# The down projection of each expert step is made between its two up projections instead of behind both

## The chip, the core and the metric

The kernel runs on one core of a Trainium2 chip. The metric is the device time of one execution in microseconds (us); the times given are medians of several executions of the same program. TensorE (PE in the profile) multiplies matrices, VectorE (DVE) and ScalarE (ACT) work element by element and copy results out of the accumulator banks (PSUM), GpSimd (POOL) issues the indirect transfers, SyncE (SP) the others.

## The reference

A block of three layers on x (8 sequences, 512 tokens, width 128): half an expert layer, a recurrent mixing layer, half an expert layer again.

```python
def _L0_ffn_ref(x, gate_w, w1, w3, w2):
    logits = jnp.einsum('btd,de->bte', x, gate_w)
    probs = jax.nn.softmax(logits, axis=-1)
    expert_weights, expert_indices = jax.lax.top_k(probs, TOP_K)          # TOP_K = 2 of E = 8
    expert_weights = expert_weights / expert_weights.sum(-1, keepdims=True)
    for i in range(E):
        wi = jnp.where(expert_indices == i, expert_weights, 0.0).sum(-1)
        h = silu(jnp.einsum('btd,df->btf', x, w1[i])) * jnp.einsum('btd,df->btf', x, w3[i])   # F = 512
        out = out + jnp.einsum('btf,fd->btd', h, w2[i]) * wi[..., None]
    return out

def _L0_attn_ref(x, ...):
    # x mixed with the token before it, three projections k, v, r, a scan over the tokens
    # with running maximum, numerator and denominator (_wkv), then
    return jnp.einsum('bsd,ed->bse', r * wkv, Wo)

x = x + 0.5 * _L0_ffn_ref(_layernorm(x), ...)
x = x + _L0_attn_ref(_layernorm(x), ...)
x = x + 0.5 * _L0_ffn_ref(_layernorm(x), ...)
```

## The kernel before

Each token goes to 2 of 8 experts. The kernel sorts the tokens by expert: GpSimd scatters their rows to `rows_in` in device memory, in tiles of 128 rows that belong to one expert each, and later gathers the results from `rows_out`. There are 177 such tiles, in nine runs (a run is a group of sequences, first for the first expert layer, then for the second). Each tile is one **step** t of the program, and all engines walk through the steps in the same order (`in_order`, L423): `tile(t)`, and behind it the extra steps that a planner (`make_plan`, L217) put behind tile t: norms, gating, counting and the whole mixing layer, cut in pieces.

What each engine does in step t, in the order of its queue:

- **TensorE** (`tile`, L1274): waits for `h` of step t-2; up projection with w1 into bank `pa` (`up`, L1236); turns the rows of the next load into `pT`, if the next step begins one (`turn_tile`, L1227); up projection with w3 into bank `pb`; down projection of step t-3 (SKEW is 3) into bank `py` (`down`, L1250), which first waits for s_yrow, that is for ScalarE's copy of the previous down projection. Then its extra steps: the k, v, r products (`project`, L1292), turns, gate logits, counts.
- **ScalarE** (`tile`, L792): copies `py` of step t-4 to `yrow` (`copy_y`, L780); copies `pT` to `rT` (L773); makes `sil` of `pa` (L798); issues the store of `yrow` to `rows_out` (L785). Then its extra steps: norms (`xn`), their high halves (`parts`), copies of the products (`kk`, `vv`, `tr`), `xT`, `xnT`, `logit`, and two exponentials (L862, L863).
- **VectorE** (`tile`, L1108): `h` = `sil` times `pb`, once both are there and the down projection of six steps ago has read its slot. Then its extra steps, up to several us of them.

`pa` and `pb` have two banks each, `py` has one. In the weights, an up projection is three float16 products for each piece (high and low parts), 12 matmuls of 128 columns, or 6 of 256 where two tiles share an expert (a paired step); a down projection is 4 float32 matmuls, each of which runs as two in the trace (8). At the start of a run TensorE loads the experts' offsets into registers (`load_experts`, L1264). After the last step TensorE waits for the last `h` and makes the last three down projections.

Of the kernel before, what the change touches and what calls it, by code (L numbers as in the profile page):

```python
# [152 lines left out]
def expert_of(t):  # L153

    run = max(r for r in range(RUNS) if START[r] <= t)
    return ESTART[run] + (TILE_OF[t][0] - QSTART[run] if PAIRS[run] else t - START[run])


def paired(t):

    return TILE_OF[t][2] == 2 and PAIRS[max(r for r in range(RUNS) if START[r] <= t)] > 0
# [250 lines left out]
def run_of(t):  # L412

    return max(r for r in range(RUNS) if START[r] <= t)


def wait(eng, sem, value):

    if not isinstance(value, int) or value > 0:
        eng.wait_ge(sem, value)  # L420
# [19 lines left out]
def macaron_kernel(nc, x, channel_vecs, att_w, gate, w1, w3, w2, out):  # L440
    with ExitStack() as ctx:
# [3 lines left out]
        def ps(name, shape, dt=F32):  # L445
            return ctx.enter_context(nc.psum_tensor(name, shape, dt))

        def sem(name):
            return ctx.enter_context(nc.semaphore(name))
# [85 lines left out]
        pb = [ps(f"pb{q}", [P, FC * T]) for q in range(2)]  # L535
# [41 lines left out]
        s_up3 = sem("w3_up_done")  # L577
# [44 lines left out]
        def _(sp):  # L622
# [64 lines left out]
            for t in range(TILES + SKEW + 1):  # L687
                if t < TILES and TILE_OF[t][1] == 0 and TILE_OF[t][0] + SLOTS < QSTART[RUNS]:
                    load(TILE_OF[t][0] + SLOTS)
                if t > SKEW:  # L690
                    sp.wait_ge(s_yrow, t - SKEW)
                if t < len(later):
                    fill(*later[t])
                for _, name, run, b in (p for p in PLAN if p[0] == t < TILES):
                    step(name, run, b)
# [187 lines left out]
        def _(dve):  # L883
# [119 lines left out]
            def place_on(run):  # L1003

                new, _, low, base, more = (ne[:, i, :] for i in range(5))
                at = count(B_STEPS, ("count", run, 0))
                dve.wait_ge(s_bfull, at)
                dve.tensor_tensor(new, bkB[:, 0:E], left[:, 1, :], ALU.subtract).then_inc(s_bread, 1)
                dve.wait_ge(s_bread, at)
                link(dve.tensor_scalar(nei[:, 0, :], new, 0.0, float(T - 1), ALU.max, ALU.add))  # L1010
                link(dve.tensor_scalar(neh[:, 0, :], nei[:, 0, :], T.bit_length() - 1, None, ALU.logical_shift_right))
                dve.tensor_copy(ends[:, 2, 0:1], ends[:, 1, E:])
                link(dve.tensor_copy(kp[:, 0, :], neh[:, 0, :]))
                link(dve.tensor_tensor_scan(ends[:, 2, 1:], one_s[:], kp[:, 0, :], 0.0, ALU.mult, ALU.add))
                link(dve.tensor_scalar(ends[:, 2, 1:], ends[:, 2, 1:], ends[:, 1, E:], None, ALU.add))
                link(dve.tensor_scalar(low, ends[:, 2, 0:E], float(T), None, ALU.mult))
                link(dve.tensor_tensor(base, low, left[:, 1, :], ALU.subtract))
                link(dve.tensor_tensor(more, left[:, 0, :], base, ALU.subtract))
# [204 lines left out]
        def _(pe):  # L1223
# [3 lines left out]
            def turn_tile(q):  # L1227
                pe.wait_ge(s_rin[q % SLOTS], 16 * (q // SLOTS + 1))
                wait(pe, s_rT, q)
                for n in range(TILE_OF[FIRST_STEP[q]][2]):  # L1230
                    for part in range(2):
                        mm = pe.transpose(pT[:, part, n * T:(n + 1) * T],  # L1232
                                          rin[:, q % SLOTS, n, part * D:(part + 1) * D], ident16[:])
                mm.then_inc(s_turn, 1)

            def up(t, bank, w):  # L1236

                q, half, _ = TILE_OF[t]
                per, own = (FC // 2, slice(0, 2 * T)) if paired(t) else (FC, slice(half * T, (half + 1) * T))
                cols = own.stop - own.start  # L1240
                for i in range(per):
                    c = half * per % FC + i
                    for k, (wp, xp) in enumerate(((0, 0), (0, 1), (1, 0))):
                        at = 2 * ((w + wp) * F + c * P)
                        mm = pe.matmul(bank[:, i * cols:(i + 1) * cols],  # L1245
                                       weight_bytes[:, bass.ds(experts[expert_of(t)] * 4 + at, 2 * P)].bitcast(F16),
                                       rT[:, q % 2, xp, own], start=(k == 0), stop=(k == 2))
                return mm

            def down(t):  # L1250

                q, block, _ = TILE_OF[t]
                cols, per = (2 * T, FC // 2) if paired(t) else (T, FC)
                wait(pe, s_yrow, t)
                for c in range(FC):
                    w = weight_bytes[:, bass.ds(experts[expert_of(t)] * 4 + 4 * (UPW + c * D), 4 * D)].bitcast(F32)
                    at = c % per * cols + (block * T if paired(t) else 0)
                    step = FIRST_STEP[q] + c // per if paired(t) else t
                    mm = pe.matmul(py[:], h[:, step % RING, at:at + T], w, start=(c == 0), stop=(c == FC - 1))  # L1259
                mm.then_inc(s_y, 1)  # L1260
# [3 lines left out]
            def load_experts(run):  # L1264

                pe.wait_ge(s_eid, run + 1)
                _, found = nc.values_load_multi_w_load_instructions(
                    eid[0:1, ESTART[run]:ESTART[run + 1]], engines=(mybir.EngineType.PE,), min_val=0,
                    max_val=(E - 1) * WORDS,
                    skip_runtime_bounds_check_because="tiles() writes a count of experts, at most E - 1, times WORDS")  # L1270
                for k in range(NE[run]):
                    experts[ESTART[run] + k] = found[k]

            def tile(t):  # L1274
                q, half, _ = TILE_OF[t]
                if t in START:
                    load_experts(run_of(t))
                if half == 0:
                    pe.wait_ge(s_rT, q + 1)
                wait(pe, s_h, t - 1)  # L1280
                up(t, pa[t % 2], 0).then_inc(s_up1, 1)
                if t + 1 < TILES and TILE_OF[t + 1][1] == 0:
                    turn_tile(TILE_OF[t + 1][0])
                up(t, pb[t % 2], 2).then_inc(s_up3, 1)
                if t >= SKEW:
                    down(t - SKEW)

            def bank_free(s_read, uses):

                wait(pe, s_read, uses - 1)  # L1290
# [68 lines left out]
            def weights_in():  # L1359
                turn_tile(0)  # L1360
                pe.wait_ge(s_uplo, E)
                pe.wait_ge(s_w2, 16 * E)

            in_order(tile, step, before_tiles=weights_in)
            pe.wait_ge(s_h, TILES)
            for t in range(TILES - SKEW, TILES):
# [28 lines left out]
```

## Time and profile before

| | |
|---|---|
| median of 3 runs | 621.75 us (621.48 to 623.04) |
| the profiled execution | 623.24 us, of which the span of its instructions is 621.4 us |
| TensorE busy | 521.1 us (84%) |
| VectorE, ScalarE, GpSimd busy | 423.8 us (68%), 318.9 us (51%), 389.3 us (63%) |
| mean granted TensorE clock | 0.97 of full speed |

How to read it: the steps begin at about 55 us, after the first routing and the loading of weights, and TensorE's last down projection starts at 596.7 us. The rest is the last gathers, their addition and the writing out. A busy share is a mean over stretches with different limits, so what a new order does is read from single steps and from the waits. In the profile, a time in brackets behind an instruction is the time for which its engine was idle before it, and what ended that. Starts are counted from the beginning of the span. The engine named PEld is TensorE's loading of weights, which overlaps its matmuls.

### The profile page before, as it was taken

Reading aid. Unit: us, or ns where it says so; the run is one execution under the profiler, and the core shown is the slowest. Engines: PE = TensorE matmul, PEld = TensorE weight load, DVE = VectorE, ACT = ScalarE, POOL = GpSimd, SP = SyncE. Lnnn points to the kernel's source line nnn. Section 1 sums busy time; section 2 is a strip of 40 time slices with the busy share of each in tenths; the row PEclk is TensorE's granted clock in tenths of the full one; section 3 lists DMA queues with packets and bytes.
Section 4 is the critical chain, followed back from the end, with each engine's and each line's share of the span. In section 5 each row is a group of like instructions: output and inputs, shape, how many; then the busy total and the mean of one; then the engine's idle time right before and its main releaser. Section 6 shows DMA issues by size and latency. Waiting matters only on the chain.

```text
span 621.4 us, 18551 instructions
## 1 busy us (share of the span) xinstructions
PE 521.1 (84%) x5866; PEld 477.7 (77%) x5866; DVE 423.8 (68%) x1218; ACT 318.9 (51%) x703; POOL 389.3 (63%) x490
## 2 busy tenths in 40 slices
PE   1235899999999899998999959998989999989930
PEld 1233789898978789877898849887879899978930
DVE  4862863556878988799998955887788765215431
ACT  5433674444585565756676534776473444434410
POOL 1171058489999970599808996003949887835973
PEclk9999899999999999999999979999998999989985
DMA  8963233544232221212221133111121442313332
GB/s 284 329 192 113 61 92 114 156 137 124 79 116 65 78 74 53 74 60 73 78 66 53 59 101 87 49 37 36 54 81 57 121 112 83 103 45 99 91 89 59
DMA packets 89062, 59.55 MB, mean 96 GB/s; under 512 B 10256, under 2 KB 82704, under 8 KB 88976
## 3 DMA queue, kind: packets, MB, share of 16 engines
q1 hardware_dynamic: 55296, 29.97, 16.5%
q0 software_dynamic: 8192, 16.79, 8.9%
q10 hardware_dynamic: 25488, 11.61, 6.5%
q8 instruction: 58, 0.95, 0.6%
q14 instruction: 28, 0.23, 0.1%
HBM read 28.65 MB, written 29.69 MB: 94 GB/s over the span
## 4 chain that ended last, share of the span: by engine, by line
PE 56%; DVE 13%; ACT 11%; issue 8%; POOL 8%; DMA 3%; POOLq 0%; ACTq 0%; DVEq 0%; SPq 0%
PE py L1259 18%; PE pa L1245 14%; PE pb L1245 12%; POOL rows_in L725 3%; ACT xn L817 3%; POOL yg L737 3%; DVE h L1114 3%; PE pT L1232 2%; PE bkB L1318 2%; PE bkB L1297 2%; ACT sil L798 2%; POOL pace L754 2%; PE bkA L1312 2%; ACT rT L778 1%; PE bkA L1297 1%
## 5 line engine op out<-in xcount | busy, mean ns | idle before, releaser
L725 POOL DMA_INDIRECT rows_in<-parts,slot x128 | 135.0, 1054 | 183.1 <-DVE slot L1039 161.2
L1114 DVE TENSOR_TENSOR h<-sil,pb 128x512 f32<-128x512 f32 x177 | 120.7, 686 | 127.3 <-ACT sil L798 79.6
L1259 PE MATMUL py<-ffn_w,h 128*128 x1416 | 198.6, 284 | 9.4 <-ACT yrow L783 9.0
L1259 PEld LDWEIGHTS py<-ffn_w,h 128*128 128x128 f32 x1416 | 175.2, 195 | 15.2 <-issue 12.3
L1245 PE MATMUL pa<-rT,ffn_w 128*128 128x128 f16 (+1 forms) x1752 | 151.7, 233 | 22.8 <-issue 12.5
L1245 PE MATMUL pb<-rT,ffn_w 128*128 128x128 f16 (+1 forms) x1752 | 154.5, 232 | 0.0
L1245 PEld LDWEIGHTS pa<-rT,ffn_w 128*128 x1752 | 124.2, 99 | 37.6 <-issue 26.4
L737 POOL DMA_INDIRECT yg<-rows_out,slot x128 | 125.4, 980 | 38.6 <-issue 22.8
L754 POOL MEMSET pace<- 128x544 uint8 x223 | 127.7, 573 | 0.1
L1245 PEld LDWEIGHTS pb<-rT,ffn_w 128*128 x1752 | 122.2, 98 | 6.8
L798 ACT ACTIVATE sil<-pa 128x512 f32<-128x512 f32 x177 | 105.3, 595 | 40.4 <-PE pa L1245 39.9
L783 ACT ACTIVATE yrow<-py 128x128 f32<-128x128 f32 x177 | 48.5, 274 | 87.2 <-PE py L1259 84.7
L778 ACT ACTIVATE rT<-pT 128x512 f16<-128x512 f16 (+1 forms) x112 | 56.8, 507 | 68.0 <-PE pT L1232 62.8
L1232 PE MATMUL pT<-ident,rin 128*128 128x128 f16 x354 | 38.6, 221 | 9.7 <-DMA rin<-rows_in 9.7
L817 ACT ACTIVATE xn<-xres,shift,rstd 128x128 f32<-128x128 f32 x96 | 39.3, 486 | 9.5 <-DVE shift L926 8.3
L1124 DVE SCALAR_TENSOR_TENSOR xres<-yg,wts,xres 128x128 f32<-128x128 f32 x120 | 34.1, 346 | 9.2 <-DMA yg<-rows_out,slot 8.6
L1312 PE MATMUL bkA<-ident,xn 128*128 128x128 f32 x64 | 11.8, 315 | 28.3 <-ACT xn L817 27.5
L1232 PEld LDWEIGHTS pT<-ident,rin 128*128 128x128 f16 x354 | 25.9, 99 | 11.0 <-DMA rin<-rows_in 10.0
L1312 PEld LDWEIGHTS bkA<-ident,xn 128*128 128x128 f32 x64 | 8.5, 165 | 29.6 <-issue 28.4
L904 DVE BATCH_NORM_STATS2 stats<-xres 128x6 f32<-128x128 f32 x96 | 20.9, 280 | 4.3 <-DMA xres<-in_x 3.9
L1297 PE MATMUL bkB<-xT,qkv_w 128*128 128x512 f16 x96 | 23.4, 379 | 0.3 <-ACT xT L847 0.3
L934 DVE TENSOR_TENSOR parts<-xn,parts 128x512 f16<-128x512 f32 x24 | 16.4, 689 | 10.6 <-ACT parts L831 10.5
(156 smaller groups left out, 459.2 us busy)
## 6 DMA issues: line engine op xcount, KB each, us to landing
rows_out<-yrow ACTq DMA_DIRECT2D x177, 64.0 KB, 1.9
rin<-rows_in SPq DMA_DIRECT2D x65, 128.0 KB
rows_in<-zrow SPq DMA_DIRECT2D x34, 128.0 KB, 2.0
shared<-in_w SPq DMA_DIRECT2D x16, 256.0 KB, 6.7
rin<-rows_in SPq DMA_DIRECT2D x47, 64.0 KB
rows_in<-zrow SPq DMA_DIRECT2D x2, 1472.0 KB, 11.0
xres<-in_x SPq DMA_DIRECT2D x4, 512.0 KB, 6.3
ffn_w<-in_w SPq DMA_DIRECT2D x8, 256.0 KB, 5.2
```

Source lines behind the costliest of these rows:

```text
L725: pool.indirect_dma_start(rows_in[g][:], bass.IndirectOffsetOnAxis(ap=slot[:, c, at:at + 1], axis=0), parts[:, at, :], None).then_inc(s_sc ...
L737: pool.indirect_dma_start(yg[:, n % GSLOTS, c, j, :], None, rows_out[SET[run]][0:PASS_STEPS[PASS[run]] * T, :], bass.IndirectOffsetOnAxis( ...
L754: pool.memset(pace[:, sent % PACES, :], 0).then_inc(s_pace, 1)
L778: act.activation(rT[:, q % 2, :, 0:n], pT[:, :, 0:n], ACT.Copy).then_inc(s_rT, 1)
L783: act.activation(yrow[:, t % YSLOTS, :], py[:], ACT.Copy).then_inc(s_yrow, 1)
L798: act.activation(sil[:, t % 2, :], pa[t % 2][:], ACT.Silu, scale=1.0 / WS).then_inc(s_sil, 1)
L817: ins = act.activation(xn[:, at, j, :], xres[:, js, :][:, j, :], ACT.Identity, bias=shift[:, u, j:j + 1], scale=rstd[:, u, j:j + 1])
L1114: dve.tensor_tensor(h[:, t % RING, :], sil[:, t % 2, :], pb[t % 2][:], ALU.mult).then_inc(s_h, 1)
L1232: mm = pe.transpose(pT[:, part, n * T:(n + 1) * T], rin[:, q % SLOTS, n, part * D:(part + 1) * D], ident16[:])
L1245: mm = pe.matmul(bank[:, i * cols:(i + 1) * cols], weight_bytes[:, bass.ds(experts[expert_of(t)] * 4 + at, 2 * P)].bitcast(F16), rT[:, q % ...
L1259: mm = pe.matmul(py[:], h[:, step % RING, at:at + T], w, start=(c == 0), stop=(c == FC - 1))
L1297: mm = pe.matmul(bank[:], qkv_w[:, f, wp, :], xT[:, u % 2, xp, start:start + S], start=(n == 0), stop=(n == 5))
```

## The change

In every step from the fourth on, TensorE makes the down projection of step t-3 before the second up projection instead of after it. The turn of the next rows keeps its place behind the first up projection, and the extra steps stay at the end.

```diff
                 up(t, pa[t % 2], 0).then_inc(s_up1, 1)
                 if t + 1 < TILES and TILE_OF[t + 1][1] == 0:
                     turn_tile(TILE_OF[t + 1][0])
-                up(t, pb[t % 2], 2).then_inc(s_up3, 1)
                 if t >= SKEW:
                     down(t - SKEW)
+                up(t, pb[t % 2], 2).then_inc(s_up3, 1)
```

The queues of the other engines stay as they are, row for row. On TensorE, the middle of step 44, behind the first up projection (`pa0`) and the turn (`pT`), reads before:

```order
1292 L1245 MATMUL pa0<-rT,ffn_w 128x128 x2
1293 L1245 REGISTER_ALU
1294 L1245 MATMUL pa0<-rT,ffn_w 128x128
1295 L1232 MATMUL pT<-ident16,rin 128x128 x2
1296 L1245 REGISTER_ALU
1297 L1245 MATMUL pb0<-rT,ffn_w 128x128 x2
1298 L1245 REGISTER_ALU
1299 L1245 MATMUL pb0<-rT,ffn_w 128x128
```

and now:

```order
1292 L1245 MATMUL pa0<-rT,ffn_w 128x128 x2
1293 L1245 REGISTER_ALU
1294 L1245 MATMUL pa0<-rT,ffn_w 128x128
1295 L1232 MATMUL pT<-ident16,rin 128x128 x2
1296 L1259 REGISTER_ALU
1297 L1259 MATMUL py<-ffn_w,h 128x128
1298 L1259 REGISTER_ALU
1299 L1259 MATMUL py<-ffn_w,h 128x128
```

The down projection (`py`), with its wait for `yrow`, has come to stand where the second up projection (`pb0`) began.

On TensorE, the end of step 40, where the k product of the mixing layer (`bkB`, L1297) is an extra step, and the beginning of step 41 (`pa1`), before:

```order
1143 L1245 MATMUL pb0<-rT,ffn_w 128x128
1144 L1259 REGISTER_ALU
1145 L1259 MATMUL py<-ffn_w,h 128x128
1146 L1259 REGISTER_ALU
1147 L1259 MATMUL py<-ffn_w,h 128x128
1148 L1259 REGISTER_ALU
1149 L1259 MATMUL py<-ffn_w,h 128x128
1150 L1259 REGISTER_ALU
1151 L1259 MATMUL py<-ffn_w,h 128x128
1152 L1297 MATMUL bkB<-xT,qkv_w 128x512 x6
1153 L1245 ISA
1154 L1245 MATMUL pa1<-rT,ffn_w 128x128 x2
```

and now:

```order
1145 L1245 MATMUL pb0<-rT,ffn_w 128x128 x2
1146 L1245 REGISTER_ALU
1147 L1245 MATMUL pb0<-rT,ffn_w 128x128
1148 L1245 REGISTER_ALU
1149 L1245 MATMUL pb0<-rT,ffn_w 128x128 x2
1150 L1245 REGISTER_ALU
1151 L1245 MATMUL pb0<-rT,ffn_w 128x128
1152 L1297 MATMUL bkB<-xT,qkv_w 128x512 x6
1153 L1245 ISA
1154 L1245 MATMUL pa1<-rT,ffn_w 128x128 x2
```

The product keeps its place in front of the next step; behind it is now the second up projection's end, where the down projection's was.

## Rows read from the trace of the kernel before

**Rows 1.** The page's busy times, share of the span and instructions of each engine.
```profile
PE 521.1 (84%) x5866; PEld 477.7 (77%) x5866; DVE 423.8 (68%) x1218; ACT 318.9 (51%) x703; POOL 389.3 (63%) x490
```

**Rows 2.** TensorE's waits, 65 to 585: us in total, times, longest.
```profile
PE pa L1245 <- issue: 12.5, 5, 6.6
PE pa L1245 <- DVE h L1114: 9.1, 9, 2.0
PE py L1259 <- ACT yrow L783: 7.5, 13, 0.9
...
PE pT L1232 <- DMA rin<-rows_in: 0.8, 1, 0.8
```

**Rows 3.** Timeline of step 17, plain: start us, us, engine, line, operation, operands.
```profile
104.04 0.83 PE L1245 MATMUL pa<-rT,ffn_w 128*128 128x128 f16 x12
104.24 0.28 ACT L783 ACTIVATE yrow<-py 128x128 f32<-128x128 f32 x1 [0.74 <-PE py L1259]
...
104.82 0.83 PE L1245 MATMUL pb<-rT,ffn_w 128*128 128x128 f16 x12
...
105.49 1.11 PE L1259 MATMUL py<-ffn_w,h 128*128 x8
105.92 0.69 DVE L1114 TENSOR_TENSOR h<-sil,pb 128x512 f32<-128x512 f32 x1 [1.71 <-ACT sil L798]
...
106.44 0.28 PE L1245 MATMUL pa<-rT,ffn_w 128*128 128x128 f16 x2
```

**Rows 4.** ScalarE's waits, 66 to 585, for the v, r and k products.
```profile
ACT vv L855 <- PE bkA L1297: 13.6, 7, 2.3
ACT tr L858 <- PE bkB L1297: 12.7, 6, 2.3
ACT kk L852 <- PE bkB L1297: 11.2, 7, 2.0
```

**Rows 5.** Timeline of step 41, behind the k product.
```profile
168.30 0.83 PE L1245 MATMUL pa<-rT,ffn_w 128*128 128x128 f16 x12
...
168.50 0.60 ACT L852 ACTIVATE kk<-bkB 128x512 f32<-128x512 f32 x1 [1.83 <-PE bkB L1297]
...
168.99 0.27 ACT L783 ACTIVATE yrow<-py 128x128 f32<-128x128 f32 x1
...
169.08 0.83 PE L1245 MATMUL pb<-rT,ffn_w 128*128 128x128 f16 x12
```

**Rows 6.** Timeline of step 44, with the exponentials.
```profile
179.32 0.83 PE L1245 MATMUL pb<-rT,ffn_w 128*128 128x128 f16 x12
179.40 1.04 ACT L863 ACTIVATE shared<-shared 128x1024 f32<-128x1024 f32 x1
...
180.35 0.26 ACT L783 ACTIVATE yrow<-py 128x128 f32<-128x128 f32 x1
...
180.73 1.13 PE L1259 MATMUL py<-ffn_w,h 128*128 x8 [0.58 <-ACT yrow L783]
```

**Rows 7.** Timelines of steps 32 and 54: TensorE's rows behind a wait for h.
```profile
144.47 0.81 PE L1245 MATMUL pa<-rT,ffn_w 128*128 128x256 f16 x6 [1.38 <-DVE h L1114]
...
210.70 0.83 PE L1245 MATMUL pa<-rT,ffn_w 128*128 128x256 f16 x6 [0.97 <-DVE h L1114]
```

**Rows 8.** Timeline of step 20, with the h of step 19.
```profile
110.72 0.69 DVE L1114 TENSOR_TENSOR h<-sil,pb 128x512 f32<-128x512 f32 x1 [1.71 <-ACT sil L798]
...
112.15 1.06 PE L1245 MATMUL pb<-rT,ffn_w 128*128 128x128 f16 x12
...
113.00 0.20 ACT L839 ACTIVATE logit<-bkB 128x32 f32<-128x32 f32 x1 [2.31 <-DVE chosen L959]
```

**Rows 9.** Stretches: us, busy of PE, PEld, DVE, ACT, POOL, granted clock, DMA share, GB/s.
```profile
144.60:149.00 4.40, 4.40 (x44) 4.15 (x43) 2.44 (x8) 1.96 (x4) 3.92 (x6) 1.00 0.47 111
...
468.70:472.00 3.30, 3.30 (x24) 3.23 (x23) 3.23 (x6) 0.28 (x1) 2.97 (x4) 0.50 0.17 60
```

**Rows 10.** Timeline of the end: last store, first of the last eight gathers.
```profile
598.14 0.33 ACTq L789 DMA_DIRECT2D rows_out<-yrow  x1
...
602.27 0.95 POOL L737 DMA_INDIRECT yg<-rows_out,slot  x1 [0.30 <-issue]
```

## What I expected of the change

> **What bounds the kernel now.** I read the busy shares first: TensorE is busy for 84% of the span, VectorE for 68%, ScalarE for 51% [rows 1]. Then TensorE's waits over the stretch of the 177 steps: after the registers are loaded at the starts of runs (12.5 us) it waited 9.1 us for `h`, 7.5 us for the copy `yrow` of the last down projection, 0.8 us for rows [rows 2]. So TensorE's order and what it waits for set the time, and the work is the same before and after. The question is only what a new order does to the waits.
>
> A plain step shows the order [rows 3]: `pa` (first up projection) starts at 104.04, `pb` (second) at 104.82, `py` (down, of three steps earlier) at 105.49, `pa` of the next step at 106.44. An up projection takes 0.67 us from start to start, the turn of the next rows 0.11, the down projection 0.95. (The busy time of 0.83 and 1.11 holds each block's end, which overlaps the next.) The step is 2.40 us.
>
> Two other engines are in the loop. **ScalarE** copies `py` into `yrow` (0.28 us), and the next down projection may not start before, as `py` is one bank. In the plain step the copy ends at 104.52 and the down projection starts at 105.49: 0.97 us of cover. **VectorE** makes `h` when both `sil` and `pb` are there; TensorE wants `h` two steps later.
>
> **The change, part by part.** No instruction is added or taken away. In steps 3 to 176 the down projection moves ahead of `pb`, so that it wants the copy 0.67 us earlier and `pb` is ready 0.95 us later.
>
> *The copy, plain steps.* The cover falls from 0.97 to 104.82 - 104.52 = 0.30 us, and grows again as the copied down projection itself ended earlier. No wait; cost 0.
>
> *The copy, where ScalarE is late.* ScalarE's queue holds the copy behind `sil` and the extra steps of the step before. Where it comes from that work to the copy without idling, the copy does not move up with the down projection. For each such step I took: end of `yrow` plus 0.13 us (the lag from its end to `py`; 180.35 + 0.26 to 180.73 is 0.12 in rounded numbers [rows 6]) minus the start of `pb`. Where this is above zero, TensorE will wait that long. Reading all 173 copies that precede a down projection in this way gives 55 steps with 36.8 us of such waits. They replace 7.9 us of waits that are there now, so 28.9 us come in. By what ScalarE did just before:
>
> - copies of the k, v and r products: 22 steps, 6.6 us, none waits now. In step 41, `pa` starts at 168.30, `kk` is copied from 168.50 and `yrow` from 168.99 to 169.26, `pb` starts at 169.08: 169.26 + 0.13 - 169.08 = 0.31 us [rows 5]. In this kind ScalarE itself waits for TensorE's product (20 times in three rows [rows 4]), and the product now stands behind `pb` as it stood behind `py`. The chain is tied to TensorE, so each loss is full: **+6.6**.
> - the two exponentials: 7 steps, 10.7 us for 4.8 now: +5.9. In step 44 the second one runs from 179.40 for 1.04 us, `yrow` ends at 180.61, `pb` starts at 179.32: a wait of 1.41 in place of 0.58 [rows 6].
> - `xT`: 6 steps, 5.8 us for 1.0 now: +4.9.
> - norms, their splits, `xnT` and `logit`: 16 steps, 10.6 us for 1.9 now: +8.6.
> - nothing but `sil`, held up by a table load after the exponentials: 4 steps, 3.0 us for 0.2 now: +2.8.
>
> *What of this is counted twice.* TensorE that has waited once arrives late at the next step and finds ScalarE no later: a cluster of waits costs its largest once. Steps 11, 45, 52, 69, 71, 77, 95 and 120 follow such a wait: -6.1, and -0.3 more in steps 69 to 71, where a product waits for `xT` anyway.
>
> *What other waits swallow.* After the exponentials of steps 51, 76 and 119, VectorE works without a pause and TensorE waits for it three steps later: 0.97 us at 210.70 [rows 7], about as much at the other two. VectorE's chain starts from ScalarE and does not move, so the lag of TensorE (0.8, 0.8 and 1.0) fits into these waits: -2.6. The wait for rows of 0.8 us [rows 2] ends with a transfer that GpSimd's own queue paces, so a later TensorE finds it over: -0.8. The sum for ScalarE is 28.9 - 6.4 - 3.4 = **+19.1 us**.
>
> *`h` is later.* In the plain step `h` started at 105.92 behind `sil`; `pb` will end at 105.65 + 0.95 = 106.60, so `h` moves by 0.7 us [rows 3], in steps without a turn by 0.9. TensorE wants it about 2.2 us after its end, so by itself this costs nothing. It costs where VectorE's work behind `h` is waited for. In step 20 ScalarE waits 2.31 us for the choice of experts, made behind the `h` of 110.72, and the copy queues behind it [rows 8]: +0.7 on the wait counted above. Of this kind are also steps 30, 36 to 39, 49, 128 and 145, at 0.3 to 0.9 each: together **+3.0**, with 0 and 9 x 0.9 = 8 as the ends.
>
> *The clock.* After long idles TensorE's granted clock fell to 0.50 (the 1.2 GHz level), as from 468.70 to 472.00, after a wait of 1.38 us it stayed at 1.00 [rows 7, 9]. Half speed over such a stretch costs half of it, 1.7 us. Waits that the change makes long are those of steps 20 (2.0 us), 94 (1.7) and 119 (1.9); others reach 1.6. I take two falls, **+3.4**; ends 0 and 8 x 1.7 = 14.
>
> The Trainium skill ("TensorE: Matmul & The Clock Gate", section "A second HAM failure mode: psum-queue depth-cycling") says that short idles between groups of matmuls can make the clock swing between its two levels. The rows here do not bear that out for single waits up to 1.4 us; by that rule the high end of this term would be the case.
>
> *The end.* `h` of the last step is no longer hidden by a down projection: the last three come 0.9 us later. The last store now goes out at 598.14 and lands 1.9 us on, GpSimd comes to the gathers that need it at 602.27 [rows 10]: 2.2 us of cover, cost 0.
>
> *Issue.* `pb` took 1.06 us in step 20 where 0.83 is usual [rows 8, 3], with nothing that it waited for: TensorE's issue runs short at the end of two up projections in a row. All such excess is 6.9 us in `pb` and 3.1 in `pa`. Between two down projections there are still two ups, now `pb` then `pa`, so I take 0; ends -7 and +5.
>
> **Sum:** 19.1 + 3.0 + 3.4 = 25.5 us. The profiled execution took 623.2 us (621.4 of span and 1.8 around it) and would take 648.7; on the median of the runs, 621.75, it is **647 us**.
>
> **The rivals.**
>
> *The waits vanish in others (634 us).* If VectorE-bound stretches swallow more than the three I counted, the ScalarE term shrinks to the tied kinds, some 12 us. For: TensorE waits for `h` in 9 places, 9.1 us in all [rows 2]. Against: most lie far from the late copies. Chance 0.16, about 628 to 638.
>
> *The clock falls often (659 us).* Eight falls in place of two add 6 x 1.7 = 10 us, and 2 more if the clusters merge less. For: four stretches at half clock are there already, each behind a long idle. Against: 1.38 us was not enough [rows 7, 9], and only three waits are clearly longer. Chance 0.15, 655 to 668. (This is the way in which the rule of the Trainium skill named above would show.)
>
> *The copy moves up too (623 us, no change).* The down projection that is copied also ends 0.67 us earlier, and if ScalarE were waiting for it everywhere, as it is in the plain step, the cover would be kept. Against: in the 55 steps ScalarE came to the copy straight from other work [rows 5, 6]. Chance 0.04.
>
> *Faster (615 us).* The mechanism is issue: the down projection is slow in the array and lets the issue get ahead, so standing between the ups it could take away the stretch of `pb`, 6.9 us, if `pa` did not stretch instead. It decides only if the late copies cost less than 6.9 us. Against: `pa` follows `pb` directly now, and the 22 tied steps alone cost 6.6. Chance 0.03.
>
> **How the numbers follow.** The sum has 0.62, 638 to 654. The range takes in most of the two slower and quicker neighbours: 632 to 660 leaves about 0.15 out. A measurement of this kernel can tell 0.3%, 2 us, from no change. Slower by more than that: 0.62 + 0.16 + 0.15 = 0.93, and 0.01 of the two small cases, 0.94; no change 0.03; faster 0.03.
>
> **What would show it.** TensorE's wait for `yrow` should grow from 7.5 us and 13 times [rows 2] to some 30 us in 40 to 50 places, now found after `pa` or the turn; its wait for `h` should stay at about 7 to 11; ScalarE's wait for `py` should fall. `pb` in the plain step should still take 0.83 us, and GpSimd's last eight gathers still follow without a gap. The sum is wrong if the waits for `yrow` stay under 15 us (then ScalarE was less tied than I read it), if the granted clock is at 0.50 in more than six stretches, or if the waits for `h` exceed 15 us (then the later `h` was the larger cost).

## The result and the profile after

The changed kernel took 645.83 us (median of four runs, 643.95 to 646.26) where the kernel before took 622.06 (four runs, 621.48 to 623.04). The ratio is 1.0375, with a 95% interval from 1.0354 to 1.0396: 3.75% slower, about 23.8 us. The profiled execution has a span of 644.5 us where it was 621.4, so 23.1 us are there to be explained.

First the busy times of the changed kernel, the same line as [rows 1]; then two of its costliest groups of instructions (behind the first bar: busy us in all, mean ns of one; behind the second: the idle time just before the group and what ended most of it):

```profile
PE 527.4 (82%) x5866; PEld 478.9 (74%) x5866; DVE 421.7 (65%) x1218; ACT 315.7 (49%) x703; POOL 387.2 (60%) x490
...
L1114 DVE TENSOR_TENSOR h<-sil,pb 128x512 f32<-128x512 f32 x177 | 121.0, 686 | 162.7 <-PE pb L1245 121.7
L1259 PE MATMUL py<-ffn_w,h 128*128 x1416 | 201.5, 287 | 25.3 <-ACT yrow L783 22.6
```

The counts of instructions are those of before. VectorE's `h` now mostly starts behind `pb` (121.7 of its 162.7 us of idle time), where it mostly started behind `sil`; the down projection has 22.6 us of idle time behind `yrow`. TensorE's waits between 65 and 608 us, to set beside [rows 2] (us in total, times, longest):

```profile
PE py L1259 <- ACT yrow L783: 21.7, 29, 2.0
PE pa L1245 <- issue: 12.1, 4, 6.9
PE pa L1245 <- DVE h L1114: 10.8, 11, 1.9
```

The wait for `yrow` was 7.5 us in 13 places and is 21.7 in 29; that for `h` went from 9.1 to 10.8; the wait of 0.8 us for gathered rows is gone. ScalarE's wait for `py` fell from 76.0 us in 95 places to 18.6 in 41. Three places show what happened. A plain step (17 again) of the changed kernel:

```profile
105.25 0.83 PE L1245 MATMUL pa<-rT,ffn_w 128*128 128x128 f16 x12
...
106.03 1.11 PE L1259 MATMUL py<-ffn_w,h 128*128 x8
...
106.98 0.83 PE L1245 MATMUL pb<-rT,ffn_w 128*128 128x128 f16 x12
107.18 0.28 ACT L783 ACTIVATE yrow<-py 128x128 f32<-128x128 f32 x1
107.65 0.83 PE L1245 MATMUL pa<-rT,ffn_w 128*128 128x128 f16 x12
```

It lasts 107.65 - 105.25 = 2.40 us, as in [rows 3]. Next, steps 40 and 41, at the two copies that [rows 5] are near to (`xT`, then `kk`):

```profile
170.39 1.02 ACT L847 ACTIVATE xT<-bkA 128x1024 f16<-128x1024 f16 x1 [1.60 <-PE bkA L1341]
...
171.31 0.27 ACT L783 ACTIVATE yrow<-py 128x128 f32<-128x128 f32 x1
...
171.71 1.13 PE L1259 MATMUL py<-ffn_w,h 128*128 x8 [0.58 <-ACT yrow L783]
...
174.85 0.60 ACT L852 ACTIVATE kk<-bkB 128x512 f32<-128x512 f32 x1 [2.50 <-PE bkB L1297]
...
175.34 0.27 ACT L783 ACTIVATE yrow<-py 128x128 f32<-128x128 f32 x1
...
175.74 1.13 PE L1259 MATMUL py<-ffn_w,h 128*128 x8
```

In both steps the down projection stands where the copy is not done yet. In step 41 `pa` starts at 174.65 and takes 0.67 us, the turn 0.11, so the down projection could start at 175.43; it starts 0.31 us later, as read off for this step, and the record shows no wait in brackets. ScalarE itself now waits longer for the k product (2.50 us where [rows 5] have 1.83): its copy of the product moves with TensorE. Last, step 44, the place of [rows 6]:

```profile
186.41 1.04 ACT L863 ACTIVATE shared<-shared 128x1024 f32<-128x1024 f32 x1
...
187.36 0.26 ACT L783 ACTIVATE yrow<-py 128x128 f32<-128x128 f32 x1
...
187.74 1.13 PE L1259 MATMUL py<-ffn_w,h 128*128 x8 [0.87 <-ACT yrow L783]
```

The wait was 0.58 and is 0.87 (and 1.39 at step 51, where it was 0.73).

**Where the 23.1 us are.** I took, for each step, the time from its first `pa` matmul to that of the next step in both traces, and summed the differences. The clock's share of a difference is taken as half the change in the time that TensorE was busy at half clock; time that it stood idle there costs nothing.

| part | forecast | measured |
|---|---|---|
| the 55 steps read off as late, without the clock (28.9, less 6.4 for clusters) | +22.5 | +20.2 |
| all other steps, without the clock (swallowed -3.4, later `h` +3.0, issue 0) | -0.4 | +1.2 |
| clock | +3.4 | +2.1 |
| before step 3 and behind step 176 | 0 | -0.5 and +0.1 |
| sum | +25.5 | +23.1 |

### The profile page after: what moved, and what is told of

Same layout as the page of the kernel before. It is cut to its first block, busy times and chain, and to the rows that moved or that the text cites. A ratio compares the mean times of both kernels' runs of the same rounds, so it can differ in the third digit from the quotient of the medians.

```text
span 644.5 us, 18551 instructions
## 1 busy us (share of the span) xinstructions
PE 527.4 (82%) x5866; PEld 478.9 (74%) x5866; DVE 421.7 (65%) x1218; ACT 315.7 (49%) x703; POOL 387.2 (60%) x490
## 4 chain that ended last, share of the span: by engine, by line
PE 51%; DVE 10%; ACT 8%; issue 8%; POOL 3%; DMA 1%; POOLq 0%; ACTq 0%; DVEq 0%
PE py L1259 18%; PE pb L1245 12%; PE pa L1245 11%; PE bkB L1297 3%; POOL yg L737 3%; DVE h L1114 2%; PE pT L1232 2%; ACT xn L817 2%; PE bkA L1297 2%; PE bkB L1318 1%; ACT sil L798 1%; ACT yrow L783 1%; PE bkA L1355 1%; DVE xres L1124 1%; ACT shared L863 1%
## 5 line engine op out<-in xcount | busy, mean ns | idle before, releaser
L725 POOL DMA_INDIRECT rows_in<-parts,slot x128 | 132.0, 1031 | 205.3 <-DVE slot L1039 183.4
L1114 DVE TENSOR_TENSOR h<-sil,pb 128x512 f32<-128x512 f32 x177 | 121.0, 686 | 162.7 <-PE pb L1245 121.7
L1259 PE MATMUL py<-ffn_w,h 128*128 x1416 | 201.5, 287 | 25.3 <-ACT yrow L783 22.6
L1245 PE MATMUL pa<-rT,ffn_w 128*128 128x128 f16 (+1 forms) x1752 | 153.3, 233 | 24.0 <-issue 12.1
L1245 PE MATMUL pb<-rT,ffn_w 128*128 128x128 f16 (+1 forms) x1752 | 150.4, 234 | 0.0
L1245 PEld LDWEIGHTS pb<-rT,ffn_w 128*128 x1752 | 126.4, 100 | 5.7
L1232 PEld LDWEIGHTS pT<-ident,rin 128*128 128x128 f16 x354 | 25.0, 98 | 10.8 <-DMA rin<-rows_in 9.0
L904 DVE BATCH_NORM_STATS2 stats<-xres 128x6 f32<-128x128 f32 x96 | 20.9, 280 | 4.3 <-DMA xres<-in_x 3.8
L1297 PE MATMUL bkB<-xT,qkv_w 128*128 128x512 f16 x96 | 23.4, 380 | 0.0
```

The source lines that it names most:

```text
L725: pool.indirect_dma_start(rows_in[g][:], bass.IndirectOffsetOnAxis(ap=slot[:, c, at:at + 1], axis=0), parts[:, at, :], None).then_inc(s_sc ...
L1114: dve.tensor_tensor(h[:, t % RING, :], sil[:, t % 2, :], pb[t % 2][:], ALU.mult).then_inc(s_h, 1)
L1232: mm = pe.transpose(pT[:, part, n * T:(n + 1) * T], rin[:, q % SLOTS, n, part * D:(part + 1) * D], ident16[:])
L1245: mm = pe.matmul(bank[:, i * cols:(i + 1) * cols], weight_bytes[:, bass.ds(experts[expert_of(t)] * 4 + at, 2 * P)].bitcast(F16), rT[:, q % ...
L1297: mm = pe.matmul(bank[:], qkv_w[:, f, wp, :], xT[:, u % 2, xp, start:start + S], start=(n == 0), stop=(n == 5))
```

## The experiments

They ran on two other chips. The two kernels again and the last two experiments ran on the one, called the second chip here, where the kernel before takes 635.4 us (eight runs, 633.8 to 637.4); the four experiments between them ran on a third, where it takes 635.5 (eight runs, 633.7 to 637.1). Most of the difference from 622 lies behind step 176 (9.0 of 11.4 us of the span, in the trace of the second chip), where each engine stands still for some microseconds. So ratios are compared, and in the traces how far a kernel lies behind the kernel before at the start of step 176. There is no trace of the kernel before from the third chip, so the traces of those four experiments are read against the one from the second, and differences of a few tenths of a microsecond between them can be the chip's.

### The two kernels again

> The kernel before, unchanged, profiled again beside its variants. Nothing is varied: its time sets how far two runs of one program on this chip lie apart (about 0.3%), and its records give the waits and durations of this chip against which the variants are read. TensorE's waits for yrow should again be 7.5 us or so at 13 places, those for h about 9 us.

> The changed kernel, unchanged, beside the kernel before. If its loss belongs to the order of the work and not to one chip, the ratio is again 1.035 to 1.040, with TensorE's waits for yrow at 20 to 23 us in some 30 places. If the loss depended on this chip's other timings (transfers, table loads), the ratio would leave 1.03 to 1.045.

The kernel before took 634.66 us with a span of 632.8; TensorE's waits were 8.2 us for `yrow` (12 places) and 7.4 for `h` (6) between 65 and 592 us. The changed kernel took 658.79 us (four runs), a ratio of 1.0374 [1.0342, 1.0405], with 9.9 us of waits for `h` between 65 and 613 us and, for `yrow`:

```profile
PE py L1259 <- ACT yrow L783: 22.1, 29, 1.8
```

The loss came back on another chip, so it belongs to the order. At step 176 the changed kernel is 20.9 us behind. The 55 late steps are 20.4 us longer without the clock, the clock is 1.4, and the other steps are 0.8 shorter; 3.0 us more come behind step 176.

### The copy moved as well, new order

```diff
             def tile(t):
-                if t > SKEW:
-                    copy_y(t - SKEW - 1)
...
                 if t > SKEW:
                     store(t - SKEW - 1)
+                if t >= SKEW:
+                    copy_y(t - SKEW)
...
```

ScalarE's loop behind the last step begins one copy later to match.

> The changed order, and ScalarE now copies the down projection of step t at the end of its own step t, behind sil and ahead of the extra steps, instead of at the start of step t+1 behind them. If the cost comes from the copy standing behind ScalarE's extra work (theory), TensorE's waits for yrow (21.7 us in 29 places in the changed kernel, and 0.16 us more at each, which the profile does not count) go almost wholly, and the time falls from 645.8 to 620 to 627 us; ScalarE's extra work starts up to 0.7 us later, which may give 3 us back. If the cost comes from pb and so h being later (rival), the time stays above 638 us, since pb is as late as in the changed kernel.

Measured: 642.63 us, a ratio of 1.0103 [1.0071, 1.0135]. In its waits, 65 to 599 us, those for `yrow` are 6.6 us, where the changed kernel has 22.1 on the second chip:

```profile
PE pa L1246 <- DVE h L1115: 9.2, 9, 1.8
PE py L1260 <- ACT yrow L783: 6.6, 6, 1.2
```

Most of the loss is therefore the place of one ScalarE instruction, 0.28 us long. But the ratio is 628.5 us at the level of 622, past the end of the expected range at 627. What was left of the waits for `yrow` sits behind the exponentials, in six places, where `sil` and its table load (1.28 us) now stand ahead of the copy, as at TensorE's down projection of step 52:

```profile
205.37 1.28 ACT L796 ACT_TABLE_LOAD   x1
...
206.66 0.60 ACT L796 ACTIVATE sil<-pa 128x512 f32<-128x512 f32 x1
207.16 0.27 ACT L783 ACTIVATE yrow<-py 128x128 f32<-128x128 f32 x1
...
207.48 1.16 PE L1260 MATMUL py<-ffn_w,h 128*128 x8 [1.17 <-ACT yrow L783]
```

### The copy moved, old order

The same edit of ScalarE on the kernel before, whose TensorE is left as it was.

> The control: TensorE's order of before, with ScalarE's copy moved in the same way. Theory: the 7.9 us of waits for yrow go, but ScalarE now idles until the down projection at the end of the step is done before it begins its extra work, up to 0.9 us in some 80 steps; 612 to 622 us. Rival: if the copy's place hardly matters, 622 within 2 us.

Measured: 651.9 us, 1.0249 [1.0207, 1.0290]: slower, and outside both the theory and the rival. TensorE waits less for `yrow` (3.8 us), but now for what ScalarE makes behind the copy (65 to 610 us):

```profile
PE pa L1246 <- ACT rT L778: 5.3, 6, 1.4
PE bkA L1313 <- ACT xn L817: 4.7, 3, 2.0
PE py L1260 <- ACT yrow L783: 3.8, 5, 1.1
```

In the old order `py` is finished only at the end of a step, and ScalarE, which works in order, stands before the copy and waits: 86.0 us in 107 places, where the kernel before has 52.4 in 66 on the second chip. Everything behind the copy starts later. The early copy suits the new order only, where `py` is done 0.67 us earlier: the place of the copy and the order belong together, and the change moved one of them.

### The new order in one part of the steps

```diff
-                up(t, pb[t % 2], 2).then_inc(s_up3, 1)
-                if t >= SKEW:
+                early = t >= SKEW and t not in LATE
+                if early:
+                    down(t - SKEW)
+                up(t, pb[t % 2], 2).then_inc(s_up3, 1)
+                if t >= SKEW and not early:
                     down(t - SKEW)
```

`LATE` holds the 55 steps of the forecast. The second kernel has `t in LATE`.

> The down projection stands between the ups only in the steps outside the 55 that were read off the trace of before as those in which ScalarE comes late to the copy (119 of 174 steps changed). Theory: no wait for yrow is added, what is left is later h and issue: 620 to 627 us. Rival (h later everywhere, or a cost in each step): the cost is spread over the steps, so two thirds of 23.8 us stay: 635 to 640 us.

> The complement: the new order only in the 55 steps read off as late. Theory: nearly all of the cost, 19 to 22 us: 638 to 645 us. Rival: a third of it, 628 to 631 us.

Measured: 643.17 us, 1.0129 [1.0091, 1.0166], for the steps outside, and 653.09 us, 1.0272 [1.0230, 1.0315], for the 55. The second lies in its range of times (+17 us at 622, so 639), though below the 19 to 22 us named with it, and has the waits that the theory wants:

```profile
PE py L1264 <- ACT yrow L788: 20.6, 29, 1.7
```

The first was expected to end at 627 at most and is at 630: a miss, and its rival, 635 at least, misses as well. Its waits for `yrow` are as before (8.1 us, 13 places). Half of the 6.7 us that it is behind at step 176 is the clock (last table); a part of the rest is `h`, as in steps 35 to 38. Without the change (the kernel before, on the second chip), then with it:

```profile
153.52 0.69 DVE L1114 TENSOR_TENSOR h<-sil,pb 128x512 f32<-128x512 f32 x1 [1.11 <-PE pb L1245]
...
157.79 0.69 DVE L1114 TENSOR_TENSOR h<-sil,pb 128x512 f32<-128x512 f32 x1
...
158.87 0.88 PE L1245 MATMUL pa<-rT,ffn_w 128*128 128x128 f16 x12
```

```profile
155.13 0.69 DVE L1119 TENSOR_TENSOR h<-sil,pb 128x512 f32<-128x512 f32 x1 [1.51 <-PE py L1264]
155.74 2.31 DVE L1129 SCALAR_TENSOR_TENSOR xres<-yg,wts,xres 128x128 f32<-128x128 f32 x8
...
159.40 0.69 DVE L1119 TENSOR_TENSOR h<-sil,pb 128x512 f32<-128x512 f32 x1
...
160.33 1.14 PE L1250 MATMUL pa<-rT,ffn_w 128*128 128x128 f16 x12 [0.52 <-issue]
```

VectorE has 3.6 us of other work behind the `h` of step 35. It begins that work 1.61 us later than in the kernel before, 0.7 of it because this kernel is as much behind there already, the rest because `pb` is later. The `h` of step 36 ends at 160.09, when TensorE has been ready for half a microsecond. The row names issue as what ended the wait; the time at which it ended is 0.24 us behind that `h`. Step 37 is 0.7 us longer by this; steps 6, 9, 50, 129 and 165 are 0.4 to 0.6 us longer, which I did not follow row by row.

### The copy ahead of `sil` behind the exponentials

The first experiment's kernel, and in the eight steps that follow an `exps`:

```diff
+                if t >= SKEW and t in AFTER_EXPS:
+                    copy_y(t - SKEW)
                 act.wait_ge(s_up1, t + 1)
...
-                if t >= SKEW:
+                if t >= SKEW and t not in AFTER_EXPS:
                     copy_y(t - SKEW)
```

> The new order with ScalarE's copy of py moved to the end of its step, as in the first experiment, except in the eight steps that follow an exps, where the copy stands ahead of the silu. In the first experiment those eight places still waited 1.1 to 1.2 us each for yrow, because there the silu with its table load stood ahead of the copy. Theory (what the new order costs is only the place of the copy in ScalarE's row, plus a small rest in h): eight places times 0.8 to 1.1 us come back, so the ratio falls from 1.010 to 0.997 to 1.002, and the waits for yrow from 6.6 us to under 2 us. Rival (those copies only hand their wait to the silu, and so to h and to the next step): the ratio stays at 1.006 to 1.012 and the waits for h grow.

Measured: 641.57 us, 1.0092 [1.0063, 1.0121], not told apart from the 1.0103 without this edit: the rival. Its waits for `yrow` between steps 3 and 176 are gone (there were six, 6.6 us in all, and not eight), as the theory had it, but they come back as waits for `h`, as the rival had it. In steps 53 and 54, behind the exponentials of step 50:

```profile
207.04 0.81 PE L1251 MATMUL pa<-rT,ffn_w 128*128 128x256 f16 x6 [0.48 <-DVE h L1120]
...
209.99 0.69 DVE L1120 TENSOR_TENSOR h<-sil,pb 128x512 f32<-128x512 f32 x1
...
210.92 0.82 PE L1251 MATMUL pa<-rT,ffn_w 128*128 128x256 f16 x6 [1.23 <-issue]
```

The second wait is put down to issue, but ends 0.24 us behind the end of `h`, like the one above. The two are 1.71 us, where the first experiment's kernel has 0.27 in step 54 and had waited 1.17 for `yrow` in step 52. Steps 78 and 79 are the same case (0.48 and 1.24).

At step 99 the kernel lies 1.0 us ahead of the kernel before, where the changed kernel is 14.0 behind and the first experiment's 2.3; of the 3.3 us between these two, 0.8 were there at step 3 already, where they still do the same, and 1.7 are a stretch at half clock. Behind step 99 this kernel loses 7.9 us. The stretch from 337 us to about step 176 in this kernel, then in the kernel before on this chip (us, busy of PE, PEld, DVE, ACT, POOL with counts, granted clock, DMA share, GB/s):

```profile
337.00:599.00 262.00, 238.92 (x2913) 223.18 (x2913) 166.69 (x429) 128.17 (x281) 169.26 (x214) 0.95 0.26 73
```

```profile
337.00:592.00 255.00, 234.05 (x2916) 219.93 (x2913) 165.91 (x428) 130.13 (x281) 167.09 (x213) 0.98 0.26 75
```

Both do the same number of matmuls in it, to three; the granted clock is 0.95 in place of 0.98. Its half-clock stretches are 23.9 us long in all, where the kernel before has 13.6: one of 13.6 us begins at 361.6 (6.8 in the kernel before), and new ones stand behind a wait for `h` of 1.85 us in step 122 and in steps 140 and 162, while two of the kernel before's are gone. TensorE is busy for 17.9 us of them, in the kernel before for 11.5, so 3.2 us of the 6.8 by which it is behind at step 176 are the clock's. The long stretch begins in a wait for gathered rows in step 100, ahead of the start of the run. The row of this kernel, then of the kernel before:

```profile
362.40 0.61 PE L1238 MATMUL pT<-ident,rin 128*128 128x128 f16 x4 [2.63 <-DMA rin<-rows_in]
```

```profile
361.50 0.40 PE L1232 MATMUL pT<-ident,rin 128*128 128x128 f16 x4 [1.23 <-DMA rin<-rows_in]
```

Step 100 is 1.65 us longer than in the kernel before. All the variants that come to it less than 9 us behind the kernel before wait 2.6 to 2.8 us for these rows; those that are 12 and 14 us behind do not wait for them. GpSimd issues its transfers there one behind the other with 0.17 us between them in both kernels, which suggests that TensorE has caught up with it. What makes the rows later than in the kernel before is not shown.

### The old order kept where `h` is late

The kernel of the last experiment, with the old order and the old place of the copy in 24 steps. TensorE's part of the edit:

```diff
+                new = t >= SKEW and t not in OLD_ORDER
+                if new:
+                    down(t - SKEW)
                 up(t, pb[t % 2], 2).then_inc(s_up3, 1)
-                if t >= SKEW:
+                if t >= SKEW and not new:
                     down(t - SKEW)
```

> As the experiment before it, with the old order (down projection last) and the old place of the copy in 24 steps in which VectorE is the last to finish h or an expert's load stands ahead: 20-22, 30, 36-39, 43, 49, 100, 101, 121, 127, 128, 138-140, 146, 147, 160, 161, 164, 165. Theory (the second part of the cost is that a later second up projection makes h later exactly where h is late already): 4 to 7 us less than that experiment, a ratio of 0.987 to 0.994, thus also below the kernel before, with the waits for h back at 9 us or less. Rival (the rest of the cost is spread over all steps, or is the clock's): no more than 2 us less.

Measured: 643.99 us, 1.0121 [1.0085, 1.0157], against 1.0092: no gain, so what the theory expected did not come. The waits for `h` did not fall:

```profile
PE pa L1255 <- DVE h L1124: 13.6, 14, 1.9
PE pa L1255 <- issue: 11.4, 5, 5.2
```

In the experiment before they are 9.3 us in 11 places, but 4.5 us more are put down to issue there, in steps 32, 54, 79 and 148, which here stand under `h` (1.23 us in step 54 there, 1.24 here). So it is 13.8 us there and 13.6 here. A step that keeps the old order hands its late copy to the next (0.58 us in step 40), and the `h` that step 38 waits for is late from step 35 on, which was outside my list. This list of steps did not take the later `h` away; whether another would is not shown.

### All of them at the start of step 176

Half-clock time is read from the granted clock between 65 us and step 176, with the time that TensorE was busy in it; the clock's share is half of what the busy time exceeds that of the kernel before by.

| kernel | ratio | behind, us | at half clock, us | busy in it, us | clock's share | rest |
|---|---|---|---|---|---|---|
| before | 1 | 0 | 13.6 | 11.5 | 0 | 0 |
| after | 1.0374 | 20.9 | 17.1 | 14.2 | 1.4 | 19.6 |
| 55 late steps alone | 1.0272 | 18.3 | 17.1 | 12.7 | 0.6 | 17.7 |
| the other steps alone | 1.0129 | 6.7 | 20.5 | 18.1 | 3.3 | 3.4 |
| new order, copy moved | 1.0103 | 6.3 | 17.1 | 13.5 | 1.0 | 5.3 |
| the same, ahead of `sil` behind `exps` | 1.0092 | 6.8 | 23.9 | 17.9 | 3.2 | 3.7 |
| the same, 24 steps in the old order | 1.0121 | 9.3 | 23.9 | 17.5 | 3.0 | 6.2 |
| old order, copy moved | 1.0249 | 17.4 | 20.5 | 18.6 | 3.5 | 13.9 |

The two halves come to 17.7 + 3.4 = 21.1 for 19.6. Moving the copy takes the rest from 19.6 to 5.3; with the copy ahead of `sil` in eight steps it is 3.7, which is not clearly better. These are single profiled executions: the kernels lie up to 0.9 us apart at step 3 already, where no change has begun (0.9 in "new order, copy moved", 0.6 in the 55 late steps, 0.5 in the 24 steps), the four from the third chip are set against a trace of the second, and one stretch of 3.4 us at half clock more or less is 1.7 us.

## Why the prediction was right, step by step

I forecast 647.0 us (632 to 660); it is 645.8. The mechanism held: most of the cost is the late copy in the 55 steps. The total is closer than its terms. On the span it was +25.5 forecast and +23.1 measured, and in that the 55 steps were 2.3 us too large, the clock 1.3 too large and the other steps 1.6 too small, so that part of the closeness is luck.

- **The copy in the plain steps, 0.** Right: step 17 takes 2.40 us in both.
- **The copy where ScalarE is late.** By kind, without the clock, on the first chip and the second: k, v and r products +6.6 forecast, +7.7 and +7.9; exponentials +5.9, measured +3.6 and +3.3; `xT` +4.9 before the clusters, measured +2.7 and +2.6; norms and their like +8.6 before the clusters, measured +6.5 and +6.9; `sil` +2.8, which the clusters were to take away, measured -0.4 and -0.3. All 55: +22.5 forecast, +20.2 and +20.4 measured. **One mis-sized step** is "they replace 7.9 us of waits that are there now". The profile counts the idle time before a block from the end of the block before it, and that end is drawn 0.16 us late (0.83 us busy for 0.67 from start to start, [rows 3]). In step 44 the down projection comes 180.73 - (179.32 + 0.67) = 0.74 us later than it could, where the row says 0.58 [rows 6]. With 0.16 more for each of the 11 waits outside the clusters, 1.8 us less come in: 22.5 becomes 20.7. An exponential step then costs 0.66 us, not 0.82 (step 51: 1.39 - 0.73 in the waits, 0.65 in the step's length). By kind it fits less well than in the sum: the exponentials, 4.8 by this, are 3.6, and the products, 6.6, are 7.7. In steps 44 and 94 a product step stands directly ahead and is 0.37 and 0.22 us longer; what is left of 0.67 is 0.30 and 0.45, their measured cost. So these two are clusters that I had not counted. The excess of the products is in part step 68, 0.60 us for the 0.20 that I read; the cause of that is not shown.
- **The same 0.16 us explains the count.** I expected some 30 us in 40 to 50 places and read 21.7 in 29. A late copy of less than 0.16 us leaves no idle time in the record, and idle times up to 0.15 us are not listed as waits, though the step is longer: step 42 is 0.33 us longer with 0.15 us of idle time, which is not among the 29.
- **Clusters.** As forecast for `sil` (steps 52 and 77), both `xT` steps (45 and 95) and step 69: 0.1 us at most each. Step 11, taken as free, cost 0.65 us.
- **Swallowed by `h`.** Steps 53 and 78 are 0.65 us shorter than before, since TensorE, late by as much, meets VectorE's bound. The row of [rows 7] at 210.70 waited 0.97 us; in the changed kernel:

```profile
219.24 0.83 PE L1245 MATMUL pa<-rT,ffn_w 128*128 128x256 f16 x6 [0.27 <-DVE h L1114]
```

  The third place gave back 0.4. So 1.7 in place of 2.6. The wait for rows vanished as forecast, and a wait of 0.61 us for `yrow` took its place in step 100.
- **Later `h`, +3.0.** The steps outside the 55, with the new order alone, cost 3.4 us besides the clock (last table), but that is less whatever shorter `pb` blocks gave back, so the term by itself was not measured. On the first chip the other steps sum to +1.2, with 1.7 swallowed, 0.2 less in step 100 and some 2.5 gained in the blocks (below); if all of that gain lay in these steps, 1.2 + 1.7 + 0.2 + 2.5 = 5.6 us are left for the later `h`, an estimate, and nearly twice the forecast. Of the places, 37 and 38 were on my list (0.7 and 0.6 us), and 126, 139 and 165 (0.5 to 0.7 us each) were not.
- **The clock, +3.4.** The half-clock time went from 17.1 to 23.9 us, +6.8, or two stretches of 3.4, as I had counted. But TensorE's busy time in it went from 14.9 to 19.1 only, so the cost is 2.1 us: in the second stretch below it is busy for 5.43 of 10.20 us, since it waits for the start of a run. Of the three waits that I named, only the one in step 20 brought a fall (1.97 us long; those in steps 94 and 119 came out at 1.35 and 1.48). The stretches of the changed kernel up to step 176 (columns as in [rows 9]):

```profile
115.90:119.30 3.40, 3.40 (x41) 3.34 (x40) 0.78 (x3) 1.07 (x4) 0.00 (x0) 0.50 0.84 237
378.80:389.00 10.20, 5.43 (x43) 5.32 (x44) 3.05 (x6) 0.87 (x2) 9.26 (x12) 0.50 0.17 45
488.00:491.30 3.30, 3.30 (x24) 3.23 (x23) 2.20 (x3) 0.87 (x2) 3.13 (x4) 0.50 0.15 45
515.30:518.70 3.40, 3.40 (x24) 3.34 (x25) 0.12 (x2) 2.90 (x7) 3.08 (x5) 0.50 0.21 58
576.80:580.10 3.30, 3.30 (x18) 2.80 (x17) 0.00 (x0) 0.87 (x2) 0.00 (x0) 0.50 0.09 25
```

  The first and the fourth are new, the second was 6.8 us, and one at 69.28 is gone. The fourth stands behind the start of a run in step 140, with a wait of 1.71 us where the kernel before has 1.21; it was not on my list. That the count of two came out is luck: on the second chip the same kernel has 3.4 us more at half clock, not 6.8, and step 20 keeps its full clock there behind a wait of 1.82 us. The rival of eight falls did not come.
- **Issue, 0 with ends of -7 and +5.** All `pb` blocks together went from 154.5 to 150.4 us and all `pa` from 151.7 to 153.3, with more of both at half clock. So some 2.5 us were gained over all steps, where I had taken 0. With the estimate above, this and the later `h` are two misses of about the same size that hide each other.
- **The end, 0.** Right on the first chip: the last store goes out at 621.55, and GpSimd's gathers follow one another, the one that needs it at the usual 0.30 us:

```profile
621.55 0.33 ACTq L789 DMA_DIRECT2D rows_out<-yrow  x1
...
625.33 0.94 POOL L737 DMA_INDIRECT yg<-rows_out,slot  x1 [0.30 <-issue]
```

  On the second chip the end is 3.0 us longer with the change. The engines stand still there in both kernels; which part of the 3.0 us belongs to the change is not shown.

The Trainium skill ("TensorE: Matmul & The Clock Gate", section "A second HAM failure mode: psum-queue depth-cycling") has the clock swing when TensorE idles briefly between groups of matmuls. With 29 waits for `yrow` of up to 2.0 us instead of 13, the changed kernel has 5 half-clock stretches up to step 176 where the kernel before had 4. In its trace each of the five begins in or behind a single wait of 1.71 us or more, and waits of 1.35 to 1.48 us in steps 51, 76, 86, 94 and 119 brought none, nor did one of 1.63 in step 166 and one of 1.91 in step 5; so there the short waits were not enough. The first experiment's kernel, with the copy moved, shows that they can be. Its clock fell at 288.70 behind two short waits in step 77, with 0.83 us of work between them:

```profile
286.01 0.83 PE L1246 MATMUL pa<-rT,ffn_w 128*128 128x256 f16 x6 [0.68 <-ACT rT L778]
288.01 1.47 PE L1260 MATMUL py<-ffn_w,h 128*128 x8 [1.17 <-ACT yrow L783]
```

```profile
288.70:292.10 3.40, 3.40 (x20) 2.59 (x19) 3.33 (x5) 0.28 (x1) 3.08 (x4) 0.50 0.21 58
```

That agrees with the Trainium skill, and says that the length of the longest wait alone, by which I chose the places, does not tell where the clock falls.

**Left open.** I have no kernel that beats the one before. Three tests were not tried: a trace of the kernel before on the third chip, the new order in the 22 tied steps alone, and the old order with only the 13 copies moved that TensorE waits for. What decides whether a wait of 1.8 us lowers the clock, when two waits of 0.68 and 1.17 once did and one of 1.48 did not, is open as well.

## What to carry to other kernels

When one engine's block moves ahead within its step, look at the single-buffered result that links it to another in-order engine: if the consumer comes to it from other work, it does not move along, and the lead of the move turns into a wait. Read the cover from the trace place by place, count a place as late even if no idle time would show, and add to each wait in the record what the block before it is drawn too long. A matching edit on the other engine (here one 0.28 us copy) took most of the loss away, and the same edit without the first one was a loss of its own. A wait taken away at one place can come back behind another engine, as the waits for `yrow` behind the exponentials did as waits for `h`: compare the time and not the one wait. And charge a stretch at half clock with the work done in it, not with its length.

## What I had not expected of the hardware

- Around the start of the run at step 101, where TensorE stands idle for 5.2 to 7.0 us and the program has it load registers, every trace has a half-clock stretch, but its length differs from trace to trace: 6.8 us in the kernel before on both chips, 10.2 in the changed one on the first and 6.8 on the second, 13.6 in the last two experiments. A stretch of 3.4 us more in which TensorE works throughout costs 1.7 us, a quarter of a per cent of this kernel.
- The same program takes longer at its end on one chip than on another: from the start of step 176 to the end of the span the kernel before takes 31.0 us on the first and 40.0 on the second, with standstills whose cause the trace does not show. In the changed kernel on the second chip VectorE stands still for 12.22 us before its last `h` (the row names no instruction of this core as what ended it):

```profile
626.87 0.69 DVE L1114 TENSOR_TENSOR h<-sil,pb 128x512 f32<-128x512 f32 x1 [12.22 <-remote]
```
